# Key chunks of 476, 512 and 512 in place of three of 500: the first chunk's addition and maximum in one operation, with a zero-extended near-bias table

## The reference

```python
x = layernorm(x + attn(x))            # causal self attention, one head of 128
x = layernorm(x + xattn(x, ctx))      # 16 heads of 8, 56 queries, 1500 keys
x = layernorm(x + ffn(x))             # 128 -> 512 (silu gate) -> 512 gelu -> 512 gelu -> 128

# xattn, the part that is changed
bias = rel_bias[bucket(key_position - query_position)]   # [heads, 56, 1500]
scores = q @ k.T + bias
weights = softmax(scores)             # needs the maximum over all 1500 keys
out = (weights @ v) @ wo
```

## Time and profile before

| | |
|---|---|
| median of 3 runs | 1100.81 us (1099.06 to 1102.6) |
| the profiled execution | 1099.21 us |
| its span (first to last instruction) | 1097.4 us |
| mean granted TensorE clock | 0.951 |
| PE busy | 965.7 us (88%) |
| DVE busy | 734.5 us (67%) |
| ACT busy | 598.9 us (55%) |
| POOL busy | 394.3 us (36%) |

### The profile page before, as it was taken

How to read it: one execution, slowest core, us unless ns; L and a number is a source line. 1 busy time by engine, 2 the same in 40 slices (tenths; PEclk the granted TensorE clock), 3 DMA queues, 4 the chain that set the end, 5 groups by cost and what they waited for, 6 DMA issues and landing times. The chain is left out here.

```text
span 1097.4 us, 25840 instructions
## 1 busy us (share of the span) xinstructions
PE 965.7 (88%) x10410; PEld 656.4 (60%) x10410; DVE 734.5 (67%) x1777; ACT 598.9 (55%) x1059; POOL 394.3 (36%) x408
## 2 busy tenths in 40 slices
PE   6384289999999999999999999999989998699997
PEld 3263156666666666666666666666666666545564
DVE  3448177788887788788887788788877784440014
ACT  2031036666666666666666666666666666252232
POOL 6034004555544445555544445555544400000000
PEclk9757579999999999999999999999999999899999
DMA  8674914655555666555556666555555520300000
GB/s 249 158 210 113 182 58 136 188 178 162 175 179 176 195 187 189 182 176 162 175 178 183 184 199 180 183 177 163 176 178 162 153 73 2 108 0 1 1 9 25
DMA packets 57200, 158.18 MB, mean 144 GB/s; under 512 B 23906, under 2 KB 35322, under 8 KB 54010
## 3 DMA queue, kind: packets, MB, share of 16 engines
q1 hardware_dynamic: 57082, 156.54, 48.8%
HBM read 112.40 MB, written 42.63 MB: 141 GB/s over the span
## 5 line engine op out<-in xcount | busy, mean ns | idle before, releaser
L100 DVE TENSOR_REDUCE cmax<-max_ps 112x1 f32<-112x500 f32 x760 | 459.6, 620 | 168.7 <-PE max_ps L94 168.0
L759 ACT ACTIVATE e_sb<-st_ps 128x896 f32<-128x896 f32 (+1 forms) x384 | 354.3, 925 | 155.9 <-DVE st_ps L704 90.5
L94 PE MATMUL max_ps<-kst,qst 111*112 111x500 bf16 x760 | 291.4, 405 | 45.5 <-DVE cmax L102 22.5
L603 PEld LDWEIGHTS st_ps<-qst,kst 114*128 114x128 bf16 (+1 forms) x3072 | 192.9, 101 | 69.7 <-issue 41.8
L805 POOL TENSOR_TENSOR kpart<-k_left,kpart 128x500 bf16<-128x500 f32 x87 | 99.1, 1139 | 355.3 <-ACT k_left L776 350.8
L603 PE MATMUL st_ps<-qst,kst 114*128 114x112 bf16 (+1 forms) x3072 | 214.7, 213 | 6.0 <-DMA qst<-nmp 4.8
L94 PEld LDWEIGHTS max_ps<-kst,qst 111*112 111x112 bf16 x760 | 91.8, 129 | 118.8 <-DVE cmax L102 46.9
L631 PE MATMUL pv_ps<-e_sb,vals 128*32 128x168 f32 (+1 forms) x3072 | 149.4, 312 | 0.3 <-ACT e_sb L759 0.3
L675 PE MATMUL misc<-wv,ctxt 128*128 128x128 f32 (+1 forms) x768 | 108.3, 285 | 6.6 <-DMA ctxt<-in_ctxT 6.6
L675 PEld LDWEIGHTS misc<-wv,ctxt 128*128 128x128 f32 (+1 forms) x768 | 100.3, 194 | 21.9 <-ACT vals L744 11.8
L631 PEld LDWEIGHTS pv_ps<-e_sb,vals 128*32 128x32 f32 (+1 forms) x3072 | 80.2, 109 | 46.9 <-issue 34.4
(11 more groups left out here) (124 smaller groups left out, 922.7 us busy)
## 6 DMA issues: line engine op xcount, KB each, us to landing
kst<-kparts SPq DMA_DIRECT2D x192, 375.0 KB, 6.2
kparts<-kpart SPq DMA_DIRECT2D x96, 375.0 KB, 2.7
ctxt<-in_ctxT SPq DMA_DIRECT2D x32, 750.0 KB, 7.2
qst<-qslots SPq DMA_DIRECT2D x192, 28.0 KB, 6.2
qslots<-qst SPq DMA_DIRECT2D x1, 2688.0 KB, 13.7
vals<-in_ctxT SPq DMA_DIRECT2D x3, 750.0 KB, 12.9
h<-in_h SPq DMA_DIRECT2D x2, 1024.0 KB, 8.1
qst<-nmp SPq DMA_DIRECT2D x96, 1.8 KB
```

Of the source, the lines that this page charges most:

```text
L94: return nc.tensor.matmul(dst[0:TT, 0:CH], m.qst[0:M_ROW, r, p, :], m.kst[0:M_ROW, r, p, c * CH:(c + 1) * CH], start=True, stop=True)
L100: ins = nc.vector.tensor_reduce(m.cmax[:, r, c, p:p + 1], src[0:TT, (NEAR if c == 0 else 0):CH], AX.X, ALU.max)
L603: mm = nc.tensor.matmul(st_ps[0:K, j % 2, p // 4, (p % 4) * TT:(p % 4 + 1) * TT], m.kst[0:AUG, u % RING, p, j * P:j * P + K], m.qst[0:AUG, ...
L759: nc.scalar.activation(e_sb[0:K, j % E_RING, :].rearrange("p (a c) -> p a c", a=2), st_ps[0:K, j % 2, :, 0:HALF], ACT.Exp).then_inc(s_ex, 1)
```

## The change

Chunks are [0, 476), [476, 988), [988, 1500). near_nat becomes 476 columns wide, cleared by a memset, with the near bias in its first 146 columns, and the first chunk is reduced by the fused operation alone. Its elementwise output, which nobody reads, becomes bf16. cmax has 3 instead of 4 entries for a pair. To make room in SBUF, `qrest` of the self attention has one group's buffer instead of four, with a wait.

```diff
+BOUND = (0, S - 2 * 512, S - 512, S)
+FIRST_CH = BOUND[1]
 def max_scores(nc, m, dst, r, c, p):
-    return nc.tensor.matmul(dst[0:TT, 0:CH], m.qst[0:M_ROW, r, p, :], m.kst[0:M_ROW, r, p, c * CH:(c + 1) * CH],
+    lo, hi = BOUND[c], BOUND[c + 1]
+    return nc.tensor.matmul(dst[0:TT, 0:hi - lo], m.qst[0:M_ROW, r, p, :], m.kst[0:M_ROW, r, p, lo:hi],
                             start=True, stop=True)
 def reduce_scores(nc, m, src, r, c, p):
-    ins = nc.vector.tensor_reduce(m.cmax[:, r, c, p:p + 1], src[0:TT, (NEAR if c == 0 else 0):CH], AX.X, ALU.max)
     if c == 0:
-        ins = nc.vector.tensor_tensor_reduce(
-            out=m.near_out[:, p % 2, :], in0=src[0:TT, 0:NEAR], in1=m.near_nat[:, p, :],
-            scale=1.0, scalar=LOWEST, op0=ALU.add, op1=ALU.max, accum_out=m.cmax[:, r, NCH, p:p + 1])
-    return ins
+        return nc.vector.tensor_tensor_reduce(
+            out=m.near_out[:, p % 2, :], in0=src[0:TT, 0:FIRST_CH], in1=m.near_nat[:, p, :],
+            scale=1.0, scalar=LOWEST, op0=ALU.add, op1=ALU.max, accum_out=m.cmax[:, r, 0, p:p + 1])
+    return nc.vector.tensor_reduce(m.cmax[:, r, c, p:p + 1], src[0:TT, 0:BOUND[c + 1] - BOUND[c]], AX.X, ALU.max)
...
-        kt, at, qrest = (sb(n, [C, NG, GT]) for n in ("kt", "at", "qrest"))
+        kt, at = (sb(n, [C, NG, GT]) for n in ("kt", "at"))
+        qrest = sb("qrest", [C, GT])
...
-            sp.wait_ge(s_mem, 2)
+            sp.wait_ge(s_mem, 3)
...
-                sp.dma_start(m.near_nat[a * T:(a + 1) * T, :, :], src[:, :, 0:NEAR]).then_inc(s_un, 16)
+                sp.dma_start(m.near_nat[a * T:(a + 1) * T, :, 0:NEAR], src[:, :, 0:NEAR]).then_inc(s_un, 16)
...
+            nc.gpsimd.memset(m.near_nat[:, :, :], 0.0).then_inc(s_mem, 1)
...
+                    if g:
+                        dve.wait_ge(s_q3, g)
-                    nc.vector.tensor_tensor(qrest[:, g, :], ps[:, 0, 0:GT], q(0), ALU.subtract).then_inc(s_qr, 1)
+                    nc.vector.tensor_tensor(qrest[:, :], ps[:, 0, 0:GT], q(0), ALU.subtract).then_inc(s_qr, 1)
...
-            m.near_out, m.cmax = ib("near_out", [TT, 2, NEAR]), ib("cmax", [TT, 2, 1 + NCH, PAIRS])
+            m.near_out, m.cmax = ib("near_out", [TT, 2, FIRST_CH], BF16), ib("cmax", [TT, 2, NCH, PAIRS])
```

More of the change, by code:

```diff
@@ L478, in _ @@
                     dve.wait_ge(s_q1, g + 1)
-                    nc.vector.tensor_tensor(qrest[:, g, :], ps[:, 0, 0:GT], q(0), ALU.subtract).then_inc(s_qr, 1)
+                    if g:
+                        dve.wait_ge(s_q3, g)
+                    nc.vector.tensor_tensor(qrest[:, :], ps[:, 0, 0:GT], q(0), ALU.subtract).then_inc(s_qr, 1)
                     dve.wait_ge(s_qr, g + 1)
-                    link(nc.vector.tensor_copy(q(1), qrest[:, g, :]))
-                    nc.vector.tensor_tensor(q(2), qrest[:, g, :], q(1), ALU.subtract).then_inc(s_q3, 1)
+                    link(nc.vector.tensor_copy(q(1), qrest[:, :]))
+                    nc.vector.tensor_tensor(q(2), qrest[:, :], q(1), ALU.subtract).then_inc(s_q3, 1)
             for n in range(HEAD_START):
@@ L1129, in build @@
             ib = lambda n, sh, dt=F32: inner.enter_context(nc.sbuf_tensor(n, sh, dt))
-            m.near_nat = ib("near_nat", [TT, PAIRS, NEAR])
+            m.near_nat = ib("near_nat", [TT, PAIRS, FIRST_CH])
             m.near_t0, m.near_t1 = ib("near_t0", [P, HT]), ib("near_t1", [NEAR - P, HT])
             m.kst, m.qst = ib("kst", [P, RING, PAIRS, S], BF16), ib("qst", [P, RING, PAIRS, TT], BF16)
-            m.near_out, m.cmax = ib("near_out", [TT, 2, NEAR]), ib("cmax", [TT, 2, 1 + NCH, PAIRS])
+            m.near_out, m.cmax = ib("near_out", [TT, 2, FIRST_CH], BF16), ib("cmax", [TT, 2, NCH, PAIRS])
             m.vals = ib("vals", [P, 2, ST, 32 * VG])
```

## The result

The changed kernel took 1094.46 us (median of 7 runs, 1090.97 to 1096.99), the kernel before 1100.81 (7 runs) beside it: a ratio of 0.9947, 95% interval 0.9927 to 0.9966. One of the 7 runs of the kernel before was a slow one (1166.12 us) and is left out of the ratio; the median of the other six is 1099.94 us. 1091.3 was predicted: 1094.46 lies inside the range for all outcomes (1087 to 1098.5) and 0.5 us above the forecast's own (1088 to 1094). The profiled execution took 1090.97 us, its span is 1089.2, its mean clock 0.950. Two more comparisons, on other chips, gave 0.9994 [0.9981, 1.0007] and 0.9969 [0.9953, 0.9985]; the mean of the three is 0.9970, which is just the 0.3% that I called the smallest difference worth a name. Within the batches the gain is the same in every profile of the changed kernel, 0.17 to 0.19 us a batch, and about half of what I worked out.

The account below looks back on a forecast made before the run. TensorE's own order sets the pace, with waits for VectorE around chunk 0. 30 x 0.32 = 9.6 us saved, 0.1 lost: -9.5 us from the median 1100.81, so 1091.3; own range 1088 to 1094, for all outcomes 1087 to 1098.5.

Parts of the forecast that it names:

- The slot: VectorE's chunk 0: a pair's time up to the accumulator read falls from 0.66 to 0.57 us, bounds 0.57 to 0.65.
- The memset: Set-up: clearing near_nat takes GpSimd 3.3 us, while it is idle; uncovered it would cost 3.3 us once.
- Behind the landing: Replay after nmp lands: L704 0.61 us after the scores' load, n8's reduction 1.00 later, n10 0.35 us earlier than now.
- the nmp rows land when they did: Scores of tile 0: the nmp landing stays at 547.94, so 0.22 us of the gain becomes a wait for a DMA.
- The landing does not swallow it all: Denies the rival that at the scores only 0.09 us a batch is gained, 2.7 us in all, 1098.1 us; chance 0.13.
- TensorE does not take the whole gain: Denies the rival that the landing moves up too and n10 comes 0.42 us earlier: 12.6 us, 1088.2 us; chance 0.08.
- The longer fused operation is not slower per column: Denies the rival of a slower fused operation on VectorE; at half rate 1.07 us, +83 us, 1184 us; chance 0.05.
- The late landing that now costs more: Rival: kst and qst loads for n0 lose 0.35 us of lead, come late and delay it; about 1103 us; chance 0.03.
- the landing rival: Rival: the nmp landing before the scores of tile 0 leaves only 0.09 us a batch, 2.7 us, 1098.1 us; chance 0.13.
- The sum: Whole kernel: thirty batches at 0.32 us save 9.6, the stretch ahead of the first batch costs 0.1: -9.5 us.

## Why the prediction was right, and where it was not

**The slot** of 0.57 us was right to the hundredth, and so were its consequences: release 0.05 us ahead of the next product, n5 and n6 earlier (0.24 and 0.34 us against the key projection, 0.22 and 0.31 said), 512-column reductions at 683 ns. The group stands at 649 ns, 0.64 was said. The memset was hidden, 3.27 us against 3.3.

**Behind the landing** the replay was right as well. The load of the scores comes 546.13 - 545.05 = 1.08 us after the end of the issue (1.07 in the earlier trace rows), L710 0.61 after the load, n8's reduction 1.01 after that.

**The step that failed** is "the nmp rows land when they did": the landing was taken as fixed because "no operation of the change feeds it". Against the key projection that starts GpSimd's chain (531.44; before, L670 at 533.39), SyncE's issue stood 11.55 us behind (542.99 - 531.44), and 11.40 before (544.79 - 533.39). My replay had the scores of tile 0 at 547.94 - 533.39 = 14.55 and n10 at 550.28 - 533.39 = 16.89. With the landing 0.15 us later these become 14.70 and 17.04; measured: 546.14 - 531.44 = 14.70 and 548.49 - 531.44 = 17.05. In this batch that is the whole difference between 0.32 and 0.18 us; over 18 batches of each profile the issue is 0.13 us later (medians 11.53 and 11.40). Of the 0.15, 0.12 lie between the start of the nmp split and the issue (1.56 against 1.44), 0.03 in GpSimd's key splits before it.

**Its cause** is an order of starts that the change itself turned round. Before, L828 started at 543.35 and x_own at 543.40: GpSimd was first, x_own took 0.65 us. The two faster slots ahead of x_own bring it forward: 541.27, ahead of L834 at 541.43. Now VectorE is first, x_own takes 0.50 (a slot of 0.42 instead of 0.58), and L834 takes 0.60 instead of 0.40. VectorE won 0.16 us. The chain that sets the landing lost 0.20 at L834 and had back the 0.09 that x_own had cost L831 before (0.48 against 0.39 for L837 now): 0.11 of the 0.12. Moving x_own away from L834 put L834 back to 0.39, L837 stayed at 0.39, and the issue came 0.23 us earlier, so this is shown and not only argued. What no run does is to give back those 0.12 us and nothing else: x_own moved alone ran into the key split, and the version that freed the landing moved rec as well. That the landing bounds the period is shown by that version (24.33), how much of the missing 0.14 it is comes from the replay. The rows held the hint: an operation of VectorE with two SBUF sources, 0.65 us for 280 columns, beside one of GpSimd with nearly the same start.

The Trainium skill ("SBUF — State Buffer", on the shared port pair) says that a VectorE operation with two SBUF sources and a GpSimd operation that reads SBUF take one port pair as a lock, the first to start keeps it, and the other blocks. The rows of seven kernels here agree: x_own 0.45 to 0.50 us where it starts first, 0.65 and 0.68 behind a short GpSimd operation, 1.12 and 1.39 behind a long one; GpSimd 0.60 instead of 0.39 and 1.40 instead of 1.14 where x_own is first. I had weighed this only for the fused operations, which read PSUM and stay within 640 to 655 ns.

**The rivals.** The landing does not swallow it all: more than 2.7 us came through within the batches. TensorE does not take the whole gain. The longer fused operation is not slower per column. The late landing that now costs more came true in its mechanism and not in its price: products now wait for query loads, which they did in neither profile of the kernel before, but for 2.5 us an execution at most, far below the 0.3 us a batch that I had asked of it. What I called the landing rival was, in part, the truth: it took 0.22 us as I had said, and 0.15 more.

**The sum.** Without late landings, 4.7 + 0.8 = 5.5 us, where 9.5 was said. By the ratios, 5.8 us were measured on the first chip (late landings, start and tail lie in that as well), 3.4 on the third, and 0.7 on the second, which is not told from nothing. So the time fell into the range with some luck: 0.18 us a batch is outside my 0.25 to 0.38, and of the range for all outcomes the part above 1094 was there for the landing rival. That the kernel is faster at all, put at 0.80, holds beyond the 0.3% on the first chip and barely on the third.

## What to carry to other kernels

When a stall of one engine is removed and the next thing to bind is a DMA landing, replay the chain of that landing as well, with the new times of the other engines, and not as a constant. List the VectorE operations with two SBUF sources and look what GpSimd has running or starts beside each; a change of 0.1 us in either can turn the order round, and then what is left of the other operation is the price. If the chain to a landing may not lose, take what it does not need out of GpSimd's order ahead of it, as the version with rec moved did (ratios 0.9945, 0.9970 and 0.9932 in three comparisons), and look at the trace again: the same edit in the kernel before cost 2.2%, and even in the changed kernel a late load turned the order in 5 batches of three profiles.

## What the runs showed of the hardware

- x_own (VectorE, two SBUF sources) and GpSimd's operations held each other up to the end of the one that started first, decided by starts 0.02 to 0.31 us apart: up to 0.94 us (x_own 1.39 against 0.45). The fused operations, with one source in PSUM, stayed within 640 to 655 ns.
- The accumulator read ran beside the next fused operation: 0.57 us from start to start at 649 ns of duration.
- Six fused operations with both fp32 sources in SBUF took 653 ns each, with one in PSUM 649.
- Where the weight load waited for nmp, it began 1.07 (last batch before) and 1.08 us (the batch shown after) behind the end of the issue; in one batch near 820 us TensorE's weight load waited 2.42 us for it in the kernel before and 2.27 in the changed one.
